# Four reorderings in a four-layer gated cross-attention kernel: combinations behind the gathering, tile 0 ahead of a meeting, norm steps, a copy

## The chip, the cores and the metric

The kernel runs on 1 core of one Trainium2 chip. The metric is the time of one execution on the device in microseconds (us); lower is better. Three runs of the kernel before took 2125.79, 2128.64 and 2129.28 us; the median is 2128.64 us.

## The reference, cut to what matters

Sixteen sequences of 56 tokens of width 256 (896 tokens, seven tiles of 128) pass through four layers. Each layer is a gated cross-attention over 16 contexts of 1500 positions of width 64, and a gated feed-forward part that is different in each layer:

```python
x = x + tanh(g_xattn[n]) * xattn_n(layernorm(x), ctx)     # n = 0..3
x = x + tanh(g_ffn[n])   * ffn_n(layernorm(x))
# ffn_0: 64 experts, top 6 (grouped router), at most 64 tokens each, relu squared, and a shared expert
xd = zeros((E, CAP + 1, D)).at[e_flat, slot].set(x[tok])           # gathering
yd = einsum('eci,edi->ecd', relu2(einsum('ecd,eid->eci', xd, w1)), w2)
out = zeros((T, D)).at[tok].add(yd[e_flat, slot] * gate)           # combination
# ffn_1: 8-bit activations, ternary weights; ffn_2: 16 experts, silu(g) * u, dense with top 6 weights
# ffn_3: rmsnorm(h), then 8 experts, top 2, and a shared expert
h = x * rsqrt(mean(x * x) + 1e-6) * rms_weight
# the end of each attention of layers 1 to 3, per tile of tokens:
out = ctx_lat.reshape(b, s, H * K) @ Wo.T                          # projection
```

Everything is computed to fp32 accuracy: a matrix product is split into three, high x high, high x low and low x high, where `H` and `L` at the end of a name mark the high and the low part.

## The kernel before

**Five programs.** TensorE, VectorE, ScalarE, GpSimd and SyncE (which issues the loads) each have a program of their own, and each runs its instructions strictly in order. They wait for one another by semaphores: `e.wait_ge(*x_out.at(n, i))` waits until `x_out` of tile i in layer n has been counted. Between two stages all five meet in `stage_end` (L968): an engine drains, adds one to `meet`, and waits until all five have done so. Whatever stands behind it on any engine waits for the last engine to come.

**Layer 0's experts.** The order of the tasks is one list, made by `sparse_order` (L226), and every engine walks it and does its own share of each task. The 64 experts go in eight groups of eight, g = 0 to 7, that is four pairs q = 4g to 4g + 3. A group is a list of fourteen steps, n = 0 to 13: `ups(g)` are the up products of the group; `pick(q)` builds on GpSimd the 0/1 selection matrix `S` of the pair (L2352, from `slot_of_t` and `slots`), which the combination uses; `disp(g + 1, 0)` and `disp(g + 1, 1)` gather the tokens of the next group on TensorE (L1666, 14 matmuls each) out of `ST` compares, `st(..., a)`, that VectorE makes (L2826) and TensorE also uses (L962 with `w_pairs`); ScalarE copies the gathered tokens out; `downs(q), downs(q + 1)` are down products, whose result VectorE and ScalarE split into `YDL` (L2846) and `YDH`; `comb(q)` adds the pair's results back to the tokens (L1709, 8 matmuls with `S`, `YDH`, `YDL`); `gturn(g + 1)` turns the gates of the next group. The combination of pair 4g + 3 stands in the group after. In the kernel before, step 6 is `comb(4g)` and step 7 is `disp(g + 1, 1)` with `st(2)`.

After every step one task of a side list is popped, which prepares the contexts of layer 1: `kt` products and subtractions (L2868 on VectorE), turns of `V` and `key_steps` (L1734 on TensorE, `key_steps` on GpSimd at L2372). `wload` and `pload` in the list are loads of weights and slots on SyncE's queue; `wload` is placed behind steps 6 and 13 by number.

**Banks.** A product of TensorE lands in one of eight PSUM banks. In the experts the upper four go round: use m takes bank 4 + m % 4 (`upper_uses`, L413), and waits until the use four before it has been copied out. Combinations add up in banks of their own; gatherings, up and down products, the turns of the gates and those of the context are uses of the upper four. `S`, `YDH` and `YDL` are rings of three: `pick(q)` waits for `comb(q - 3)`.

**Projection of the attentions.** `pe_project` (L1572) goes over the seven tiles of tokens, one product of 24 matmuls each (L962, `MH`, `ML` by `CH`, `CL`) into bank i % 3. ScalarE makes `CH` (L2025), and GpSimd or VectorE the low part `CL` (L2030, `low_part`, L2027): all tiles of layer 1 and tile 0 of the others by GpSimd, the rest of layers 2 and 3 by VectorE; in layers 1 to 3 tile 0's `CH` and `CL` are made ahead of the stage. `dve_project` (L2619) adds the product to `X`, and makes mean and scale (`mv`, `shift`, `rstd`). `TURN_BEHIND[n]` says by how many tiles TensorE's turn of the normed tokens `Y` (`pe_project_turn`, L1591, matmul with `ident`) follows the projection, `LOGITS_BEHIND[n]` the same for the router's product (`pe_logits`). In layer 3 there is a second norm: ScalarE squares (`act_square`, L2074), VectorE makes `rr` from the sums `ss`, GpSimd raises it to a power (`pool_rms`, L2318, the operation at L2321), and VectorE multiplies (L2664, in `dve_rms`, L2652) before TensorE turns the tile at L1220. GpSimd also splits weights there (`WL`, L2326). The projections of layers 1 to 3 stand behind such a meeting (L1828); the last thing that TensorE does before it is the last values product of the attention (L1551, `E`, `V`).

**Experts of layers 2 and 3.** `act_experts` (L2096) walks the list of its layer. The first task of a unit (n, c) is two products of TensorE (`pe_up`, L1613, `YH` by `WH` at L962), `up(n, c)` in the list; ScalarE takes the first of them through silu out of its bank into `R` (`act_up`, L2088, the activation at L2093), VectorE multiplies `R` by the second (L2801, `HF`). In the task `gate(n, c)` ScalarE rounds `HF` to `HH` and GpSimd makes `HL` (L2342) for the down product.

## Time and profile before

| | kernel before |
|---|---|
| runs | 2125.79, 2128.64, 2129.28 us |
| median | 2128.64 us |
| profiled execution, its own time | 2128.17 us |
| its span in the trace | 2126.4 us |
| TensorE matmuls (PE) busy | 2040.6 us, 96% |
| TensorE weight loads (PEld) busy | 1422.9 us, 67% |
| VectorE (DVE) busy | 1485.2 us, 70% |
| ScalarE (ACT) busy | 1074.6 us, 51% |
| GpSimd (POOL) busy | 1359.4 us, 64% |
| mean granted TensorE clock, share of full speed | 0.994 |

The span is the stretch from the first to the last instruction that the profiler recorded, in one execution; all places in the trace are told in us from its start. The execution's own time is 1.8 us longer. Busy shares are means over very different stages, so what an engine's time is worth must be read at the place. TensorE's ends are modelled, to some tenths of a us. In a row of a timeline the numbers are the start and the length, and the bracket at the end is how long the engine stood idle before it and which instruction's end released it.

### The profile page before, as it was taken

The page shows a single profiled execution, that of the slowest core. Times are in us where ns is not written, and L with a number is a line of the kernel's source. Part 1 is how long each engine was busy: PE and PEld are TensorE (multiplying, and loading weights), DVE is VectorE, ACT ScalarE, POOL GpSimd, SP SyncE. Part 2 cuts the span into 40 slices and gives each one's busy share as a digit, 9 for nine tenths or more (in the row PEclk, how much of TensorE's full clock was granted, in tenths as well). Part 3 has the DMA queues.
Part 4 walks back from the last instruction along what each step waited for, and adds up shares of the span by engine and source line. Part 5 has one row for each costly group of instructions (what it writes and reads, how often), then busy time and mean ns, then how long its engine had stood idle before and what let it go on. Part 6 is the DMA issues. An engine that isn't in the chain of part 4 may idle for free.

```text
span 2126.4 us, 35215 instructions
## 1 busy us (share of the span) xinstructions
PE 2040.6 (96%) x13564; PEld 1422.9 (67%) x13568; DVE 1485.2 (70%) x2141; ACT 1074.6 (51%) x1770; POOL 1359.4 (64%) x850
## 2 busy tenths in 40 slices
PE   7998999999999998999999999999999999999998
PEld 5787777765565556766555655588897655655588
DVE  6869871588888857666788888653335888888653
ACT  4552332565665656211665665544434656656543
POOL 0368873188788785454788788634441887887644
PEclk9999999999999999999999999999999999999999
DMA  3035776423223104102223222025533232231022
GB/s 99 11 119 178 248 240 202 96 59 88 59 59 88 45 31 140 26 1 63 59 64 83 59 64 68 22 79 156 149 91 78 59 88 59 59 88 45 33 54 72
DMA packets 65704, 179.59 MB, mean 84 GB/s; under 512 B 11280, under 2 KB 21280, under 8 KB 65154
## 3 DMA queue, kind: packets, MB, share of 16 engines
q1 hardware_dynamic: 65154, 177.01, 31.5%
q8 instruction: 109, 1.79, 0.4%
q14 instruction: 57, 0.47, 0.1%
q10 hardware_dynamic: 384, 0.33, 0.1%
HBM read 162.32 MB, written 14.98 MB: 83 GB/s over the span
## 4 chain that ended last, share of the span: by engine, by line
PE 80%; DVE 7%; ACT 5%; POOL 3%; issue 3%; DMA 1%; POOLq 0%; DVEq 0%; SPq 0%; ACTq 0%
PE psum L962 20%; PE psum L1551 19%; PE psum L1537 18%; PE psum L1425 5%; PE psum L1436 3%; ACT E L2011 3%; PE psum L976 3%; PE psum L1709 3%; PE psum L1568 2%; PE psum L1666 2%; PE psum L1354 1%; POOL CL L2030 1%; PE psum L1252 1%; PE psum L1232 1%; DVE ST L2826 1%
## 5 line engine op out<-in xcount | busy, mean ns | idle before, releaser
L2563 DVE TENSOR_REDUCE mx<-psum 128x2 f32<-128x1000 f32 (+1 forms) x540 | 552.5, 1066 | 164.2 <-PE psum L1425 161.7
L2292 POOL TENSOR_TENSOR SA<-SA,E 125x896 f32<-125x896 f32 x288 | 606.3, 2105 | 19.0
L2011 ACT ACTIVATE E<-psum 125x896 f32<-125x896 f32 x576 | 512.7, 918 | 101.2 <-PE psum L1537 83.2
L1551 PE MATMUL psum<-E,V 125*64 125x448 f32 x2304 | 449.4, 539 | 0.0
L1551 PEld LDWEIGHTS psum<-E,V 125*64 125x64 f32 x2304 | 163.4, 137 | 246.4 <-issue 239.0
L1537 PE MATMUL psum<-QH,KH 64*125 64x448 f32 x1152 | 255.3, 399 | 10.2 <-ACT E L2011 4.2
L1537 PE MATMUL psum<-QL,KH 64*125 64x448 f32 x1152 | 241.4, 365 | 0.0
L2292 POOL TENSOR_TENSOR SA<-E,E 125x896 f32<-125x896 f32 x48 | 101.5, 2115 | 200.3 <-PE psum L1425 152.1
L1537 PE MATMUL psum<-QH,KL 64*125 64x448 f32 x1152 | 228.1, 363 | 0.0
L1425 PE MATMUL psum<-KH,QH 64*128 64x500 f32 x864 | 182.0, 405 | 1.8 <-ACT QR L1953 1.6
L2585 DVE RECIPROCAL RS<-psum 128x448 f32<-128x448 f32 x48 | 142.0, 2957 | 46.0 <-PE psum L1568 45.5
L2342 POOL TENSOR_TENSOR HL<-HF,HH 128x448 fp32r<-128x448 f32 x70 | 81.2, 1164 | 129.9 <-ACT HH L2116 129.8
L1537 PEld LDWEIGHTS psum<-QH,KH 64*125 64x125 f32 x1152 | 111.0, 181 | 78.2 <-ACT E L2011 57.3
L1537 PEld LDWEIGHTS psum<-QL,KH 64*125 64x125 f32 x1152 | 128.7, 182 | 6.5
L2801 DVE TENSOR_TENSOR HF<-R,psum 128x448 f32<-128x448 f32 x62 | 38.3, 620 | 128.9 <-PE psum L962 109.6
L1537 PEld LDWEIGHTS psum<-QH,KL 64*125 64x125 f32 x1152 | 124.5, 183 | 3.5
L1425 PEld LDWEIGHTS psum<-KH,QH 64*128 64x128 f32 x864 | 88.2, 185 | 51.1 <-issue 35.8
L1436 PE MATMUL psum<-KH,QD 64*128 64x500 f32 x270 | 121.9, 452 | 0.0
L2000 ACT ACTIVATE OB<-psum 128x448 f32<-128x448 f32 x45 | 24.5, 545 | 183.0 <-PE psum L1551 183.0
L1991 ACT ACTIVATE M<-psum,bd 128x128 fp32r<-128x128 f32 x192 | 54.7, 367 | 119.8 <-PE psum L1510 119.8
L2292 POOL TENSOR_TENSOR SA<-SA,SB 125x896 f32<-125x896 f32 x45 | 104.3, 2319 | 14.0 <-DVE SB L2581 13.5
L2352 POOL TENSOR_SCALAR S<-slot_of_t,slots 128x896 fp32r<-128x896 bf16 x32 | 92.9, 2906 | 31.8 <-PE psum L1709 17.0
(310 smaller groups left out, 4302.1 us busy)
## 6 DMA issues: line engine op xcount, KB each, us to landing
KH<-kt_scratch SPq DMA_DIRECT2D x96, 375.0 KB, 5.3
KL<-kt_scratch SPq DMA_DIRECT2D x96, 375.0 KB, 7.1
EW<-in_f_w SPq DMA_DIRECT2D x64, 256.0 KB, 5.9
kt_scratch<-kt SPq DMA_DIRECT2D x16, 750.0 KB, 6.4
WS<-in_f_w SPq DMA_DIRECT2D x31, 384.0 KB, 4.7
GB<-gates_scratch SPq DMA_DIRECT2D x36, 224.0 KB, 3.8
slot_of_t<-slots_scratch SPq DMA_DIRECT2D x64, 112.0 KB, 4.4
WoT<-in_a_WoT SPq DMA_DIRECT2D x24, 256.0 KB, 3.4
```

The costliest lines, as they stand in the source:

```text
L962: i = e.matmul(o, a, b, start=start and n == 0, stop=stop and n == len(pairs) - 1, **kw)
L976: e.matmul(psum[:, bank, 0:P], ident[:, :], ident[:, :], start=True, stop=True)
L1425: return e.matmul(psum[:, bank, 0:CW], QH[b % 3][rows, q:q + P], KH[b % 3][rows, c * CW:(c + 1) * CW], start=c == 0, stop=True, skip_group ...
L1436: return e.matmul(psum[:, 5, 0:CW], QD[b % 2][rows, :], KH[b % 3][rows, c * CW:(c + 1) * CW], start=(c, odd) == (0, 0), stop=True, skip_gr ...
L1537: i = e.matmul(psum[0:LP, pair + odd, 0:HT], keys[rows, which], queries[rows, odd * shift:odd * shift + HT], start=kind == "head" and x == ...
L1551: i = e.matmul(psum[c * DC:(c + 1) * DC, 4, 0:HT], V[0:LP, b, tile * DC:(tile + 1) * DC], E[g[n, b, k] % NE][0:LP, half[c]], start=k == 0, ...
L2011: e.activation(E[m % NE][0:LP, :].rearrange("p (c q) -> p c q", c=2), psum[0:LP, pair:pair + 2, 0:HT], ACT.Exp).then_inc(exp_set.sem, 1)
L2292: e.tensor_tensor(SA[b % 2][0:LP, :], a[0:LP, :], x[0:LP, :], ALU.add).then_inc(sum_set.sem, 1)
L2342: e.tensor_tensor(m["HL"][u][:, :], m["HF"][u][:, :], m["HH"][u][:, :].bitcast(F32), ALU.subtract).then_inc(hl_set.sem, 1)
L2352: e.tensor_scalar(m["S"][q % 3][:, :], m["PB"][q % 3][:, :], m["slots"][:, CAP0:CAP0 + 1], None, ALU.is_equal).then_inc(s_set.sem, 1)
L2563: e.tensor_reduce(o, psum[:, max_banks(kind, *t), 0:CW], AX.X, ALU.max).then_inc(small_free.sem, 1)
L2585: e.reciprocal(RS[:, :], psum[:, small_bank(kind, b), 0:HT]).then_inc(small_free.sem, 1)
```

## The change

Four things are moved; nothing is computed in another way.

1. In each group of layer 0's experts, `comb(4g)` and the step with `disp(g + 1, 1)` and `st(2)` change places. The side list's tasks keep their step numbers, and so do the loads.
2. In layers 1 to 3 the product of projection tile 0 is issued by TensorE before the meeting instead of behind it, into bank 6 instead of bank 0, and VectorE reads it from there. Tile 3, which used to wait for tile 0 to be read out of bank 0, no longer waits.
3. In layer 3's projection the turn of a normed tile follows the projection by three tiles instead of four, the router's product by five instead of six, and GpSimd's and VectorE's steps of the second norm come one tile earlier.
4. In layer 2's experts ScalarE takes the first product of unit (2, 0) out of its bank before it takes up the rounding of unit (0, 0), instead of behind it: `R` of unit (2, 0) is made first.

```diff
@@ -258,8 +258,8 @@
         pick = lambda q: [("pick", q)] + ([("pload", q + 3)] if q + 3 < E0 // 2 else [])
         steps = [([("gsl", 0)] if g == 0 else []) + [("ups", g)] + (pick(0) if g == 0 else []), pick(q) if g > 0 else [("gturn", 0)],
                  [("comb", q - 1)] if g > 0 else [], ([("disp", g + 1, 0)] if more else []) + st(0) + (pick(1) if g == 0 else []),
-                 [("downs", q), ("downs", q + 1)], (pick(q + 1) if g > 0 else []) + st(1), [("comb", q)],
-                 ([("disp", g + 1, 1)] if more else []) + st(2), [("downs", q + 2), ("downs", q + 3)],
+                 [("downs", q), ("downs", q + 1)], (pick(q + 1) if g > 0 else []) + st(1),
+                 ([("disp", g + 1, 1)] if more else []) + st(2), [("comb", q)], [("downs", q + 2), ("downs", q + 3)],
                  pick(q + 2), [("comb", q + 1)] + st(3),
                  [("gsl", g + 1)] if more else [], pick(q + 3), [("comb", q + 2)] + ([("gturn", g + 1)] if more else [])]
         for n, step in enumerate(steps):
@@ -397,10 +397,10 @@
     return [t for t in CORES[n] if n != 2 or not ahead(t)]
 
 
-TURN_BEHIND = {0: 2, 1: 0, 2: 2, 3: 4}
+TURN_BEHIND = {0: 2, 1: 0, 2: 2, 3: 3}
 SPLIT_AT = {0: 3, 2: 1, 3: 1}
 EARLY_UP = {2: 5, 3: 4}
-LOGITS_BEHIND = {0: 2, 1: 0, 2: 3, 3: 6}
+LOGITS_BEHIND = {0: 2, 1: 0, 2: 3, 3: 5}
 TURNED_NORM = {0: 1, 2: 5, 3: 8}
 MADE = (slice(0, 3 * P), slice(3 * P, T))
 BACK = {0: ((0, 1), (2,)), 1: ((3, 4), (5, 6))}
@@ -1572,14 +1572,8 @@
     def pe_project(e, n):
         behind = TURN_BEHIND[n]
         for i in range(NT + LOGITS_BEHIND[n]):
-            if i < NT:
-                e.wait_ge(*low_flag(n, i).at(n, i))
-                if i >= 3:
-                    e.wait_ge(*x_out.at(n, i - 3))
-                pairs = []
-                for m in range(H // 2):
-                    pairs += split_pairs(CH[i % 3][:, m, :], CL[i % 3][:, m, :], MH[:, m, :], ML[:, m, :])
-                product(e, psum[:, i % 3, 0:D], pairs).then_inc(projected.sem, 1)
+            if (1 if n > 0 else 0) <= i < NT:
+                pe_project_tile(e, n, i)
             if behind and 0 <= i - behind < NT:
                 pe_project_turn(e, n, i - behind)
             if n in (2, 3) and i >= LOGITS_BEHIND[n]:
@@ -1587,6 +1581,19 @@
             if n in (2, 3) and i - behind == EARLY_UP[n]:
                 e.wait_ge(*yl_set.at(TURNED_NORM[n], 3))
                 pe_up(e, n, 0, 0)
+
+    def project_bank(n, i):
+
+        return 6 if n > 0 and i == 0 else i % 3
+
+    def pe_project_tile(e, n, i):
+        e.wait_ge(*low_flag(n, i).at(n, i))
+        if i >= 3 and (n == 0 or i > 3):
+            e.wait_ge(*x_out.at(n, i - 3))
+        pairs = []
+        for m in range(H // 2):
+            pairs += split_pairs(CH[i % 3][:, m, :], CL[i % 3][:, m, :], MH[:, m, :], ML[:, m, :])
+        product(e, psum[:, project_bank(n, i), 0:D], pairs).then_inc(projected.sem, 1)
 
     def pe_project_turn(e, n, i):
         r = TURNED_NORM[n]
@@ -1825,6 +1832,7 @@
             else:
                 pe_core(e, n, behind_rope(n, lambda t: t in first_maxima(PRODUCTS_AHEAD)))
             if n > 0:
+                pe_project_tile(e, n, 0)
                 stage_end(e, next(met))
             pe_project(e, n)
             pe_stage_end(e, next(met), 3 if n < 2 else 6, (5, 22, 6, 5)[n])
@@ -2100,11 +2108,13 @@
                 if t[0] >= 2:
                     act_split(e, f, t[0])
             elif kind == "up":
-                if not swiglu or t != [0, 0]:
+                if not swiglu or t != [0, 0] and (f, t) != (2, [2, 0]):
                     act_up(e, f, *t)
             elif kind == "gate":
                 n, c = t
                 x = 2 * n + c
+                if (f, x) == (2, 0):
+                    act_up(e, f, 2, 0)
                 if not swiglu:
                     e.wait_ge(*r_set.at(f, n, c))
                     if x >= 4:
@@ -2310,9 +2320,9 @@
             pool_scales(e, 1 + 2 * n, i)
             if n != 1 and i - SPLIT_AT[n] in (0, 1):
                 pool_split(e, n, i - SPLIT_AT[n])
-            if n == 3 and i >= 2:
-                pool_rms(e, i - 2)
-        for i in (NT - 2, NT - 1) if n == 3 else ():
+            if n == 3 and i >= 1:
+                pool_rms(e, i - 1)
+        for i in (NT - 1,) if n == 3 else ():
             pool_rms(e, i)
 
     def pool_rms(e, i):
@@ -2625,7 +2635,7 @@
                 low_part(e, n, i + 2)
             if i < NT:
                 e.wait_ge(*projected.at(n, i))
-                e.scalar_tensor_tensor(X[:, i, :], psum[:, i % 3, 0:D], tanh_g[:, n:n + 1], X[:, i, :], ALU.mult,
+                e.scalar_tensor_tensor(X[:, i, :], psum[:, project_bank(n, i), 0:D], tanh_g[:, n:n + 1], X[:, i, :], ALU.mult,
                                        ALU.add).then_inc(x_out.sem, 1)
                 e.wait_ge(*x_out.at(n, i))
                 dve_stats(e, r, i)
@@ -2652,17 +2662,17 @@
     def dve_rms(e, k):
 
         m = ffn[3]
-        i = k - 2
+        i = k - 1
         if 0 <= i < NT:
             e.wait_ge(*sq_set.at(i))
             e.tensor_scalar(m["rr"][:, i:i + 1], m["ss"][:, i:i + 1], 1.0 / D, 1e-6, ALU.mult, ALU.add).then_inc(ms_set.sem, 1)
-        i = k - 3
+        i = k - 2
         if i == 0:
             e.wait_ge(*rms_in_w.at())
         if 0 <= i < NT:
             e.wait_ge(*rms_set.at(i))
             e.scalar_tensor_tensor(Y[:, i, :], Y[:, i, :], m["rr"][:, i:i + 1], m["rw"][:, :], ALU.mult, ALU.mult).then_inc(z_set.sem, 1)
-        i = k - 5
+        i = k - 4
         if i >= 0:
             dve_turn(e, 8, i, 4 + i % 4)
```

## Rows read from the trace of the kernel before

**Rows 1.** Waits of TensorE: engine, line, waited for: us, times, longest.
```profile
PE psum L1709 <- DVE YDL L2846: 9.9, 7, 2.8
PE psum L962 <- DVEq L970: 4.9, 3, 1.6
...
PE psum L962 <- ACT R L2093: 2.4, 1, 2.4
```

**Rows 2.** Windows, layer 0's experts: stretch, length, PE, PEld, DVE, ACT, POOL busy.
```profile
175.70:247.50 71.80, 63.79 (x346) 49.05 (x345) 62.76 (x80) 25.30 (x52) 71.80 (x36) 0.93 0.74 231
248.00:345.00 97.00, 91.84 (x536) 72.37 (x534) 60.51 (x88) 31.39 (x65) 65.90 (x34) 1.00 0.78 242
```

**Rows 3.** Timeline of TensorE, first matmuls of comb(0), comb(6), comb(8), comb(10).
```profile
185.87 0.74 PE L1709 MATMUL psum<-S,YDH 128*128 128x448 f32 x1 [2.79 <-DVE YDL L2846]
...
221.49 0.45 PE L1709 MATMUL psum<-S,YDH 128*128 128x448 f32 x1
...
236.12 0.47 PE L1709 MATMUL psum<-S,YDH 128*128 128x448 f32 x1 [1.71 <-DVE YDL L2846]
...
248.00 0.45 PE L1709 MATMUL psum<-S,YDH 128*128 128x448 f32 x1
```

**Rows 4.** Chain that ended last: start, us, what; two gatherings, projection tiles 4, 5.
```profile
229.68 3.25 PE psum L1666 x14
...
238.65 4.18 PE psum L1666 x14
...
2026.88 3.90 PE psum L962 x24
...
2031.00 2.83 PE psum L962 x24
```

**Rows 5.** Timeline of GpSimd, the selection matrices of pairs 5, 6 and 9, 10.
```profile
208.69 4.28 POOL L2352 TENSOR_SCALAR S<-slot_of_t,slots 128x896 fp32r<-128x896 bf16 x1
...
217.99 3.23 POOL L2352 TENSOR_SCALAR S<-slot_of_t,slots 128x896 fp32r<-128x896 bf16 x1
...
242.51 5.02 POOL L2352 TENSOR_SCALAR S<-slot_of_t,slots 128x896 fp32r<-128x896 bf16 x2
```

**Rows 6.** Timeline of VectorE, the context's subtractions in groups 0 and 5.
```profile
184.19 1.11 DVE L2868 TENSOR_TENSOR kt<-psum,kt 64x375 fp32r<-64x375 f32 x2
...
309.71 1.11 DVE L2868 TENSOR_TENSOR kt<-psum,kt 64x375 fp32r<-64x375 f32 x2 [2.51 <-ACT kt L2161]
```

**Rows 7.** Timelines at the meetings before the projections of layers 1 and 2.
```profile
781.73 2.42 PE L1551 MATMUL psum<-E,V 125*64 125x448 f32 x12
785.76 0.39 PE L962 MATMUL psum<-MH,CH 128*128 128x256 f32 x1 [1.60 <-DVEq L970]
...
786.94 4.75 POOL L2030 TENSOR_TENSOR CL<-QR,CH 128x1024 fp32r<-128x1024 f32 x2 [5.56 <-ACT CH L2025]
...
789.38 0.39 PE L962 MATMUL psum<-MH,CH 128*128 128x256 f32 x1 [0.53 <-POOL CL L2030]
...
1389.52 0.25 PE L962 MATMUL psum<-gate_hi,YH 128*128 128x16 f32 x1 [1.04 <-DVE YL L2443]
```

**Rows 8.** Timeline of layer 3's projection, VectorE's norm and TensorE's first turn.
```profile
2021.28 0.14 DVE L2435 TENSOR_SCALAR rstd<-mv 128x1 f32<-128x1 f32 x1
...
2025.66 0.48 DVE L2664 SCALAR_TENSOR_TENSOR Y<-Y,rr,rms_w 128x256 f32<-128x256 f32 x1 [1.66 <-POOL rr L2321]
...
2026.20 0.69 PE L1220 MATMUL psum<-ident,Y 128*128 128x128 f32 x2 [2.99 <-DVE Y L2664]
```

**Rows 9.** Timeline of layer 2's experts around up(2, 0) and up(3, 0).
```profile
1427.53 0.47 PE L962 MATMUL psum<-YH,WH 128*128 128x448 f32 x1 [2.36 <-ACT R L2093]
1427.66 0.62 DVE L2801 TENSOR_TENSOR HF<-R,psum 128x448 f32<-128x448 f32 x1 [1.95 <-POOL HL L2342]
...
1431.24 0.42 DVE L2448 TENSOR_TENSOR ML<-psum,MH 128x256 fp32r<-128x256 f32 x1 [0.91 <-ACT MH L1854]
...
1432.44 0.45 PE L962 MATMUL psum<-YH,WH 128*128 128x448 f32 x1
```

## The prediction, written before the changed kernel was built or timed

> **What bounds the kernel now.** I read the table of waits of TensorE first, because TensorE is busy for 2040.6 of the 2126.4 us: the time falls only where TensorE stands still or runs at the lower clock, and the reader should see that no single wait is above 0.5% of the span. Four of its waits belong to the places that the change touches [rows 1]: the combinations of layer 0's experts wait 9.9 us in seven pieces for `YDL`; the first projection tile of layers 1 to 3 waits 4.9 us in three pieces for VectorE to reach the end of the stage; the turn of layer 3's normed tokens waits 2.99 us for `Y` [rows 8]; an up product of layer 2's experts waits 2.4 us for ScalarE's copy `R`. That is 20.2 us, 0.95%. Then come the windows of the eight expert groups of layer 0, to see who else is full there: from 175.7 to 247.5 us (groups 0 to 2) GpSimd is busy for 71.80 of 71.80 us, from 248.0 to 345.0 us for 65.90 of 97.00 [rows 2]. After that only timelines, place by place.
>
> **Part 1, combinations behind the gathering.** In each group but the last, TensorE stalls at the first combination, comb(4g), and the gathering disp(g+1,1) that follows it needs nothing of it. The stalls are 2.79 and 1.71 us in groups 0 and 2 [rows 3], and 0.97, 1.88, 0.39, 1.40 and 0.73 us in the others (with these two the 9.9 us of [rows 1]). A gathering takes 3.25 us at 2.4 GHz [rows 4], more than any of the stalls, so wherever it may start at once it covers the whole stall. Whether it may start hangs on its PSUM bank, which it takes from the use four places back. In groups 1, 2, 3, 4 and 6 that use is by then the previous gathering or the up product, copied out long before. In groups 0 and 5 it is a turn of the context, which VectorE frees with the second of two `kt` subtractions: at 184.19 + 1.11 = 185.30 us, and at 309.71 + 1.11 = 310.82 us [rows 6]. TensorE would be there at 183.1 and 310.0, so there only some 0.5 us each is won. Sum: 0.97 + 1.71 + 1.88 + 0.39 + 0.73 + 2 x 0.5 = 6.7 us. In group 2 the stall is followed by a stretch at 1.2 GHz, where a gathering takes 4.18 instead of 3.25 us and half of the combination before it is slow too [rows 4]; without the stall that is up to 1.6 us more: 8.3 us.
>
> GpSimd does not let all of it through. It builds the selection matrices `S` and has no gap until 247.5 us. `S` of comb(6) ends at 217.99 + 3.23 = 221.22 us and comb(6) starts at 221.49 [rows 3, 5]: 0.27 us is all that may be kept up to there, and what groups 0 and 1 give (1.5 us) comes back as a wait for `S`. `S` of comb(10) ends at 242.51 + 2.51 = 245.02 us against a start at 248.00 [rows 3, 5]: at most 2.98 us is kept by then, of the 0.27 + 1.71 + 1.6 = 3.6. In group 3 another 1.88 us comes, less about 1 us for `S` and for the `kt` chain of VectorE, which moves only as far as the others let it (this is chosen between 0 and 2); in group 4 0.3, in groups 5 and 6 0.5 + 0.7. I take 2.98 + 1.88 - 1.0 + 0.3 + 0.5 + 0.7 = 5.4, less 0.8 for the weights and slots that must land earlier (no row shows it; between 0 and 2, near the lower end since TensorE waits for no load here) = **4.6 us gained**. Bounds: 1 us, if GpSimd's timeline binds beyond group 2, and 8.3 us. What moves along: comb(4g) ends later by 3.25 us less the stall, and behind it stand GpSimd's `S` of comb(4g+3) and ScalarE's `YDH`. In group 5 that `S` starts right at comb(20)'s end, but comb(23) is 11 us later, so nobody waits. The ST compare on VectorE and the copy of the gathered tokens on ScalarE overtake one step of the context; no DMA changes its place in SP's queue. In group 7 nothing is gathered and comb(28) only changes places with a fold product: nothing, as TensorE has no gap there.
>
> **Part 2, tile 0 of the projection ahead of the meeting (layers 1 to 3).** Today TensorE ends its last values product at 781.73 + 2.42 = 784.15 us, waits 1.60 us for the other engines, and does tile 0 from 785.76 [rows 7]. A tile takes 2.83 us from start to start, 3.1 to its last end [rows 4]. Moved ahead, tile 0 runs from 784.0 to 787.1, and only then does TensorE reach the meeting. All five engines wait there, so the meeting moves from 785.73 to about 787.1: **1.4 us later**. Queued behind it are ScalarE's `CH` of tile 1 and then GpSimd's `CL` of tile 1, which starts 1.2 us after the meeting and takes 2.37 us; tile 1 waits for that already today, at 789.38 [rows 7]. So tile 1 starts at 789.38 + 1.4, and the work moved ahead is bought with a gap of 3.6 us behind it. In layer 2 the first gate product waits 1.04 us for VectorE's chain that begins at the meeting [rows 7], and in layer 3 the turn waits for the same chain [rows 8], so the 0.4 us by which their tiles 1 to 3 come nearer to the meeting is lost there. Cost: 3 x 1.4 = **4.2 us lost**. Bounds: 2.8 us, if TensorE's end is modelled too late by half a microsecond, and 8 us, if the new gaps of 3.6, 2.4 and 2.4 us each bring the lower clock and nothing behind them hides it. I stay with 4.2, since what is slow at the start of these stages is followed by waits that absorb it. That tile 3 no longer waits for its bank and tile 0 uses bank 6 costs nothing: tile 3 doesn't wait now, and bank 6 is idle after the last maxima.
>
> **Part 3, norm steps one tile earlier (layer 3).** Today the normed tile 0 (L2664) comes in the slot after tile 3's statistics, at 2025.66, and TensorE waits 2.99 us for it [rows 8]. After the change that slot carries tile 1 and the slot before it, after tile 2's statistics at 2021.28 + 0.14 [rows 8], tile 0. TensorE then turns tile 0 at about 2021.9 instead of 2026.20, does tile 4, and waits again for tile 1's norm, which is still held by GpSimd (`rr`, behind its `WL` of block 1) until the same 2025.66. So tile 5 starts where it starts now. What is won is the turn of tile 1 (0.35 us), and the slow clock of tile 5, 3.90 against 2.83 us [rows 4], if the gap that is cut in two (some 2.6 and 1.3 us) does not lower the clock again at a place where it counts. From there to the stage's end TensorE is full. VectorE's new wait for the squares of tile 0 holds only the cast of the gate weights, 1 us before it would idle anyway. I take **0.9 us gained**, between -0.5 and 2.
>
> **Part 4, the U copy (layer 2's experts).** TensorE's 2.36 us for `R` goes, as ScalarE can make it at about 1422 instead of 1426.96, before it waits for the gate. Next late is `HL` of GpSimd (VectorE waits for it to 1427.66) for the down product, and after it the bank of up(3,0), free at 1431.24 + 0.42 = 1431.66, where up(3,0) starts now at 1432.44 [rows 9]. So 0.78 us at most is kept: **0.7 us gained**, between 0 and 2.4.
>
> **Sum.** -4.6 + 4.2 - 0.9 - 0.7 = -2.0 us. The profiled execution took 2128.17 us, so 2126.2; the median 2128.64 is 0.47 above it: **2126.6 us**, 0.1% less. Less than about 0.2% (4.3 us) a measurement of this kernel can't tell from no change: three runs of it lie 3.5 us apart.
>
> **Rivals.** (a) *GpSimd does not bind*: its `S` took 4.28 us beside VectorE's work and 2.51 us alone [rows 5], and if the new order spreads the two better, part 1 gives its 8.3 us and parts 3 and 4 their upper half: 2128.6 - 8.3 - 2.2 + 4.2 = 2122.3. For it: 15 us of GpSimd's time there are such stretching. Against: the same instructions meet in the same time. (b) *GpSimd is the bound of layer 0's groups*: its whole timeline up to group 4 stands, the stalls for `YDL` become stalls for `S`, and part 1 gives only what lies behind it, about 1.6 us; 2128.6 - 1.6 - 1.6 + 4.2 = 2129.6. For it: 71.80 of 71.80 us; against: the gaps from 248 us on [rows 2]. The Trainium skill (Perfetto Trace Analysis, Identifying the Most-Contended Engine) would have me take the busy share of GpSimd at face value and TensorE's not, and gain nothing while GpSimd is full; by that rule the time is this rival's. The same notes (GPSIMD Engine Reference, Key points) say that GpSimd shares its SBUF interfaces with VectorE's instructions of two SBUF inputs; if that is the stretching, (a) would need VectorE to do less, not the same earlier. (c) *The meeting costs more than the stalls give*, slower: the gaps of 3.6, 2.4 and 2.4 us behind tile 0 end in the lower clock, as the stall of 1.71 us did in group 2. At 1.07 us for a slow tile [rows 4], and two slow tiles in each layer, that is 4.2 + 6.4 = 10.6 us lost against 1.6 + 4.6 = 6.2: 2133.0. It decides if tile 1 and tile 2 both start at half clock and the chain of VectorE or GpSimd isn't later than they are. (d) *Part 1 does nothing*, if the gathering waits for its bank in all groups: 2126.6 + 4.6 = 2131.2; the order of the bank uses speaks against it.
>
> **Chances.** Forecast 0.50 (2124.4 to 2129.0); (a) 0.22; (b) 0.14; (c) 0.10; (d) 0.04. The range that should hold 8 in 10 reaches to the middle of (a) and of (c): 2121.5 to 2132.0. Faster by over 0.2% (below 2124.4): (a) nearly whole and a tail of the forecast, 0.28. Slower by over 0.2% (above 2132.9): half of (c) and a bit of (d), 0.07. Within: 0.65.
>
> **What would show it.** Part 1: TensorE's wait for `YDL` falls from 9.9 to about 2 us (groups 0 and 5, before the gathering now), and a wait for `S` of 1 to 2 us stands at comb(6). Part 2: no wait before tile 0, but waits of some 3.6 and 2.4 us before tile 1, and the distance from the last values product to tile 1's start grows by 1.4 us in each layer. Part 3: waits of about 2.6 and 1.3 us for `Y` instead of 2.99. Part 4: no wait for `R`, and one of 1 to 2 us behind it. I am wrong if the meeting does not move, if comb(6) doesn't wait, or if the clock falls at other places for more than 7 us.

## The result and the profile after

| | before | after |
|---|---|---|
| median of the runs taken side by side | 2126.97 us (6 runs) | 2133.90 us (6 runs) |
| ratio | | 1.0032, 95% interval 1.0017 to 1.0047 |
| profiled execution, its own time | 2128.17 us | 2135.80 us |
| its span | 2126.4 us | 2134.0 us |
| TensorE busy | 2040.6 us | 2046.9 us |
| mean granted clock | 0.994 | 0.991 |

The changed kernel is slower by 0.32%, 6.9 us. The forecast was 2 us less than before (2126.6), with a range that ended at 2132.0.

Where the time goes is read from VectorE. It runs the same 2504 recorded instructions in both kernels (those of its sequencer counted in), so the start of its n-th instruction after, less that of the n-th before, can be taken everywhere. This difference is called the shift in what follows. It is worked out from the two traces, in us, at places of the span of before (medians over five instructions; nothing is changed ahead of 130 us, so the first entry is the scatter of the start):

```
place of before   130    500    780 |  830    880  1375 | 1412 | 1427  1445  2000 | 2012   2124
shift after      0.40  -0.07  -0.12   2.01   4.17  4.19   6.56   6.11  7.07  7.02   8.50   7.61
```

Part 1 (130 to 500) gains 0.5 us. The projections of layer 1 (780 to 830) and of layer 2 (1375 to 1412) lose 2.1 and 2.4, the meeting of layer 3 (2000 to 2012) 1.5, of which part 3 gives 0.9 back. Part 4 (1412 to 1445) gains 0.45 and loses 0.96. Between 830 and 880, where nothing was changed, another 2.2 is lost.

In the waits of TensorE after (columns as in [rows 1]) the 9.9 us for `YDL`, the 4.9 for the meeting and the 2.4 for `R` are gone, and this stands in their place:

```profile
PE psum L962 <- POOL CL L2038: 3.8, 1, 3.8
...
PE psum L1673 <- DVE kt L2878: 3.0, 2, 2.1
...
PE psum L962 <- DVE kt L2878: 2.7, 2, 2.5
PE psum L962 <- SPq L970: 2.6, 1, 2.6
PE psum L962 <- DVE CL L2038: 2.6, 1, 2.6
PE psum L1220 <- DVE Y L2674: 2.4, 2, 1.6
...
PE psum L1716 <- POOL S L2362: 2.2, 3, 1.2
...
PE psum L962 <- DVE ML L2458: 1.9, 1, 1.9
```

The 3.8, 2.6 and 2.6 us are the gaps behind tile 0 in the three projections. The place in layer 1, of TensorE, SyncE's queue and GpSimd (answers to [rows 7]):

```profile
781.55 2.42 PE L1551 MATMUL psum<-E,V 125*64 125x448 f32 x12
783.91 0.39 PE L962 MATMUL psum<-MH,CH 128*128 128x256 f32 x1
...
787.08 1.29 SPq L1085 DMA_DIRECT2D wq<-wq_scratch  x3
...
788.28 2.35 POOL L2038 TENSOR_TENSOR CL<-QR,CH 128x1024 fp32r<-128x1024 f32 x1 [7.02 <-ACT CH L2033]
...
790.78 0.55 PE L962 MATMUL psum<-MH,CH 128*128 128x256 f32 x1 [3.78 <-POOL CL L2038]
791.14 0.42 PE L962 MATMUL psum<-ML,CH 128*128 128x256 f32 x1
791.35 0.41 PE L962 MATMUL psum<-MH,CL 128*128 128x256 f32 x1
```

The meeting is over at 787.08 instead of 785.73, `CL` of tile 1 starts 1.2 us behind it, tile 1 at 790.78 instead of 789.38, and its products take 0.41 us each where those of tile 0 took 0.28: the lower clock. From the end of TensorE's last values product (784.15 us before, 783.97 after) to the end of the meeting it is 1.6 us before and 3.1 us after, and the traces give the same two numbers in layers 2 and 3. So the meeting comes 1.5 us later in each of the three layers.

In layer 0's groups the two waits for the selection matrix `S` that the prediction placed are there, at comb(6) and comb(10):

```profile
221.15 0.44 PE L1716 MATMUL psum<-S,YDH 128*128 128x448 f32 x1 [0.57 <-POOL S L2362]
...
245.13 0.45 PE L1716 MATMUL psum<-S,YDH 128*128 128x448 f32 x1 [0.45 <-POOL S L2362]
```

comb(10) comes 2.87 us earlier than in [rows 3], against 2.98 forecast. But in groups 4 and 5 it is lost: comb(15) is still 2.9 us early, comb(19) is 1.5 us late. The chain that ended last has a DMA there, where the chain of before had TensorE:

```profile
271.24 3.22 POOL S L2362
277.65 9.93 DMA kt_scratch<-kt
295.11 2.94 PE psum L962 x7
```

`kt_scratch<-kt` is the store (`cstore`) with which SyncE writes a finished context's keys to memory. There are two buffers `kt`, so ScalarE's copies of context b wait until the store of context b - 2 has landed. ScalarE's copies before, then after:

```profile
276.96 0.97 ACT L2161 ACTIVATE kt<-psum 64x375 fp32r<-64x375 f32 x2 [2.99 <-DMA kt_scratch<-kt]
...
287.22 0.97 ACT L2161 ACTIVATE kt<-psum 64x375 fp32r<-64x375 f32 x2 [1.67 <-DMA kt_scratch<-kt]
```

```profile
276.62 0.98 ACT L2171 ACTIVATE kt<-psum 64x375 fp32r<-64x375 f32 x2 [6.97 <-DMA kt_scratch<-kt]
...
287.67 0.97 ACT L2171 ACTIVATE kt<-psum 64x375 fp32r<-64x375 f32 x2 [5.00 <-DMA kt_scratch<-kt]
```

The copies start within 0.5 us of where they did before; only the waits have grown, from 2.99 and 1.67 to 6.97 and 5.00 us. ScalarE came earlier, the store did not. SyncE's queue after shows what is issued ahead of each of the two stores, 1 MB of weights in four loads (`EW`):

```profile
263.92 2.01 SPq L1137 DMA_DIRECT2D EW<-in_f_w  x4
266.36 0.33 SPq L1157 DMA_DIRECT2D kt_scratch<-kt  x1
...
275.60 2.01 SPq L1137 DMA_DIRECT2D EW<-in_f_w  x4
277.65 0.43 SPq L1157 DMA_DIRECT2D kt_scratch<-kt  x1
```

### The profile page after: what moved, and what is told of

Read it like the earlier page. It is cut to its first block, busy times and chain, and to the rows that moved or that the text cites. A ratio compares the mean times of both kernels' runs of the same rounds, so it can differ in the third digit from the quotient of the medians.

```text
span 2134.0 us, 35216 instructions
## 1 busy us (share of the span) xinstructions
PE 2046.9 (96%) x13568; PEld 1425.6 (67%) x13568; DVE 1484.9 (70%) x2141; ACT 1075.7 (50%) x1770; POOL 1360.1 (64%) x850
## 4 chain that ended last, share of the span: by engine, by line
PE 76%; POOL 6%; DVE 5%; ACT 5%; issue 3%; DMA 2%; SPq 0%; PEld 0%; PEldq 0%; POOLq 0%; DVEq 0%; ACTq 0%
PE psum L962 20%; PE psum L1551 19%; PE psum L1537 18%; PE psum L1425 5%; PE psum L1436 3%; ACT E L2019 3%; PE psum L976 3%; PE psum L1568 2%; POOL S L2362 1%; PE psum L1716 1%; PE psum L1354 1%; PE psum L1673 1%; PE psum L1232 1%; POOL key_steps L2382 1%; PE psum L1252 1%
## 5 line engine op out<-in xcount | busy, mean ns | idle before, releaser
L1537 PE MATMUL psum<-QH,KH 64*125 64x448 f32 x1152 | 255.4, 400 | 10.2 <-ACT E L2019 4.0
```

The source lines that it names most:

```text
L1537: i = e.matmul(psum[0:LP, pair + odd, 0:HT], keys[rows, which], queries[rows, odd * shift:odd * shift + HT], start=kind == "head" and x == ...
```

## The experiments

Each kernel's median is of 7 to 12 runs. Ratios are to the kernel before on the same chip in the same rounds, with 95% intervals; in us they are taken of 2127.

### Each part alone

Diffs: the hunks of the change that belong to the part, on the kernel before.

> Only part 1 (comb(4g) behind disp(g+1,1)), all else as before. Theory K (the stores of the context's keys bind): TensorE is 2.9 us ahead by comb(11), as in the changed kernel, and gives all of it back by comb(18), because ScalarE's kt of context 11 and 12 still waits for the same store kt_scratch to land; the time is within 1 us of before (-0.5 us). Rival P (the predicted sum holds and part 1's gain was only lost in the changed kernel by something that parts 2 to 4 brought): 4.6 us less than before. Rival H (part 1 brings a stretch at the lower clock of its own at 295 us): 1 to 2 us more than before.

> Only part 3 (norm steps and turns one tile earlier in layer 3). Theory: TensorE waits twice (2 and 1 us) instead of once 2.99 us, and the projection of layer 3 ends 0.5 to 1.5 us earlier: 0.9 us less than before, too little to be told from no change. Rival: the gap cut in two brings the lower clock at a place where TensorE is full, 0.5 to 1 us more than before.

> Only part 2 (projection tile 0 ahead of the meeting, layers 1 to 3). Theory M (meeting later and clock): the meeting comes 1.4 us later in each layer and tile 1 waits 3.8, 2.6 and 2.6 us; tile 1 then runs at 1.2 GHz in at least two of the layers, which costs about 1 us each more, and one more stretch at the lower clock follows some 70 us behind in layer 1; together 5 to 8 us more than before. Rival N (only the later meeting costs, what follows absorbs the slow tiles): 4.2 us more. Rival O (the changed kernel's loss came from elsewhere): within 1 us of before.

> Only part 4 (R of unit (2,0) ahead of HH of unit (0,0)). Theory: the wait for R goes, but the load of the gates GB, which VectorE waits for, lands at the same time, so 0.45 us is won by 1426 us of the span, as in the changed kernel, and then the stretch at 1.2 GHz, which lay in TensorE's wait, falls where TensorE is full and takes 0.9 us: within 0.5 us of before. Rival (the prediction): 0.7 us less.

| kernel | median | ratio | in us |
|---|---|---|---|
| part 1 alone | 2126.39 | 0.9993 (0.9983 to 1.0004) | -1.5 (-3.6 to +0.9) |
| part 2 alone | 2134.25 | 1.0032 (1.0020 to 1.0043) | +6.8 (+4.3 to +9.1) |
| part 3 alone | 2125.99 | 0.9994 (0.9983 to 1.0004) | -1.3 (-3.6 to +0.9) |
| part 4 alone | 2127.43 | 1.0000 (0.9989 to 1.0010) | 0.0 (-2.3 to +2.1) |

(Median of before 2127.13.) Part 2 alone has a loss of the size of the whole; no other part can be told from no change. Part 1 alone shows the same course as in the changed kernel: comb(11) 3.2 us early, comb(19) 1.9 us late, ScalarE's two copies of `kt` at 276.60 and 288.03 us. In the trace of part 4 alone 0.8 us is won between 1412 and 1445 us, as forecast; its whole time doesn't show it.

### Part 1: what takes the 2.9 us back

The first pair of kernels, with part 1 and without it, puts loads of weights behind the stores; the second pair takes bytes away.

```diff
+    for first in (36, 40, 44, 48):              # at the end of sparse_order
+        batch = [("wload", e) for e in range(first, first + 4)]
...
+        while order[at][0] != "cstore":
+            at += 1
+        at += 2 if order[at + 1][0] == "cload" else 1
+        order[at:at] = batch
```

> Part 1, and in SyncE's list the four batches of weight loads for experts 36 to 51 stand behind the next store of the context's keys (and the context load that goes with it) instead of ahead of it; nothing is left out. Theory K (the store kt_scratch lands late because 1 MB of weights is issued ahead of it): the two stores that took 10 us to land take 5 to 7, ScalarE's kt no longer waits 5 and 7 us, and TensorE keeps the 2.9 us of groups 0 to 2 and some of its stalls of groups 4 and 5: 3 to 4.5 us less than before. Rival G (VectorE or GpSimd would be late at the same place anyway): what part 1 gives alone, 0.7 us less than before. Rival W (the weights come late instead and the up products of groups 4 to 6 wait): 1 us or more above before.

> The moved loads alone, combinations as before. Theory K: before, only 0.8 us of TensorE's time at 295 us hangs on the store, and the rest is stalls for YDL, so 0 to 1 us less than before. If it gives as much as the run with both (3 us or more), then part 1 has no part in that gain.

Measured: with part 1 ratio 1.0009 (0.9997 to 1.0020), 1.9 us more than before, but with an interval that takes in no change; alone 1.0010 (1.0001 to 1.0019), 2.1 us more. The mechanism of rival W is there. The stores land in 5.3 and 5.8 us, and ScalarE's two long waits for them are gone, but the weights are late instead: TensorE waits in the up products of group 4, where it had no wait for weights in the trace of before.

```profile
277.68 3.68 PE L970 MATMUL psum<-XD,EW 128*128 128x64 f32 x16 [3.13 <-DMA EW<-in_f_w]
```

So here the order of the queue only chose who was late.

The second pair loads only the first half of the weights of experts 32 to 47, the up weights; their down weights are left out.

```diff
-                e.dma_start(m["EW"][x % 12][:, :], io["f0_w"][NS0 + x])...
+                cut = 256 if 32 <= x < 48 else 512
+                e.dma_start(m["EW"][x % 12][:, 0:cut], io["f0_w"][NS0 + x][:, 0:cut])...
```

> Part 1, and of the weights of experts 32 to 47 only the first half (the up weights) is loaded, so the outputs of those experts are not computed with their own down weights; all else is as before. Theory K2 (in groups 3 and 4 the DMA engines are the bound: context stores and weight loads together fill them, and whichever is issued later lands late): both land in time, TensorE keeps the 2.9 us of groups 0 to 2 and adds stalls of groups 3 and 4; against the run with half loads alone it is 3 to 4.5 us faster. Rival G (VectorE and GpSimd bind there): the gap between the two is the 0.7 us that part 1 gives with full loads.

> Half loads of experts 32 to 47 alone (only their up weights are loaded, the down weights are left out), combinations as before. Theory K2: TensorE's stalls for YDL stay, only the 0.8 us wait for kt at 295 us goes: 0 to 1 us less than before. Rival: DMA binds before too, then 2 us or more less.

Measured: part 1 with half loads 0.9974 (0.9964 to 0.9984), 5.5 us less than before; half loads alone 0.9999 (0.9990 to 1.0007), nothing. The gap is 5.3 us (2.5 to 8, an estimate from the two intervals), where part 1 with full loads gives 1.5: K2 as told, and somewhat above its 3 to 4.5. comb(17), 1.5 us early with part 1 alone, is 4.0 us early, and comb(31), 0.3 us late with part 1 alone, is 5.9 us early. The two stores took this long from their issue to their landing:

| kernel | store issued at 266 to 267 us | store issued at 277 to 280 us |
|---|---|---|
| before | 10.2 us | 7.2 us |
| after | 10.2 us | 9.9 us |
| part 1 alone | 10.3 us | 10.5 us |
| part 1, loads behind | 5.3 us | 5.8 us |
| part 1, half loads | 6.6 us | 4.2 us |

The windows of part 1 alone and of part 1 with half loads from 255 to 300 us (stretch, length, PE, PEld, DVE, ACT, POOL busy, clock, DMA share, GB/s):

```profile
255.00:300.00 45.00, 39.36 (x214) 29.56 (x214) 35.83 (x50) 16.81 (x35) 37.39 (x21) 0.96 0.75 235
```

```profile
255.00:300.00 45.00, 44.16 (x265) 34.83 (x264) 40.45 (x55) 17.57 (x37) 43.01 (x22) 1.00 0.59 197
```

TensorE is busy 44.16 instead of 39.36 of 45 us, with GpSimd at 43.01. ScalarE's one wait of over 1 us for a store in this window is this; it ends 4 us earlier than with full loads:

```profile
272.56 0.97 ACT L2162 ACTIVATE kt<-psum 64x375 fp32r<-64x375 f32 x2 [2.71 <-DMA kt_scratch<-kt]
```

### Part 2: the late meeting, the gap, the clock

There are six kernels. `c_early_count` and `c_count_only` count TensorE at the meeting first:

```diff
             if n > 0:
-                pe_project_tile(e, n, 0)
-                stage_end(e, next(met))
+                e.drain().then_inc(meet.sem, 1)
+                pe_project_tile(e, n, 0)
+                e.wait_ge(meet.sem, 5 * next(met))
```

`c_early_count` and `c_parts_only` make tile 1's parts before the meeting too, and in layers 2 and 3 GpSimd makes the `CL` of tile 1 there instead of VectorE (parts of the edit, comments added):

```diff
-        return n == 1 or i == 0 or (n == 0 and i % 2 == 0)
+        return n == 1 or i == 0 or (n == 0 and i % 2 == 0) or (n > 1 and i == 1)    # low_by_pool
...
                 act_part(e, n, 0)        # ScalarE, before stage_end, n > 0
+                act_part(e, n, 1)        # waits for the last scores and for o_divided(n, 4)
...
                 low_part(e, n, 0)        # GpSimd, before stage_end
+                low_part(e, n, 1)
```

The filled kernels `c_filled` and `c_filled_fit` are part 2 with `pe_stage_end(e, next(met), 0, BUSY[n])` behind tile 0, which lets TensorE make throw-away products while it waits at the meeting, and `late_meeting` has `pe_busy(e, 6, 13)`, 13 such products, ahead of `stage_end` in the kernel before.

> The kernel before, and in layers 1 to 3 TensorE does 13 throw-away products (0.232 us each, 3.0 us) between its last values product and the meeting, so that it comes to the meeting 1.4 us after the others, as in part 2, but without a gap behind tile 0 and with nothing moved. Theory M (the meeting's delay has a price of its own): 3 x 1.4 = 4 us more than before, and what part 2 takes beyond that (to 7.1) is the gap behind tile 0 with its slow tiles. Rival Q (the delay is absorbed behind the meeting, part 2 loses by the gaps alone): within 1 us of before. Rival R (the delay costs all): 7 us more.

Measured: 2133.12 against 2127.16, ratio 1.0024 (1.0014 to 1.0034), 5.1 us more (3.0 to 7.2). The delay alone, with no gap and nothing moved, costs most of what part 2 costs: theory M, and a little above its 4. The meeting is over 3.15 us behind the last values product in each layer, 1.55 us later than before, and the shift grows by 1.6, 1.6 and 1.5 us in the three layers: in this trace a late meeting costs just its delay. The last values product, the fill, tile 0 and tile 1 in layer 1:

```profile
782.11 2.42 PE L1551 MATMUL psum<-E,V 125*64 125x448 f32 x12
784.47 3.17 PE L976 MATMUL psum<-ident 128*128 128x128 f32 x26
787.90 0.36 PE L962 MATMUL psum<-MH,CH 128*128 128x256 f32 x1 [0.26 <-PEq L970]
791.35 0.39 PE L962 MATMUL psum<-MH,CH 128*128 128x256 f32 x1 [0.38 <-POOL CL L2031]
```

> TensorE counts itself at the meeting, then does tile 0, then waits; CH and CL of tile 1 stay behind the meeting. Theory M: the meeting is back at its time, tile 1 starts at 789.4 as before (it waits for its CL), so nothing is lost and nothing won but for a gap of 2.3 us: within 1 us of before. Rival S (gap and slow tiles are most of part 2's loss): 2 to 3 us more, as these stay.

Measured: 1.0004 (0.9994 to 1.0014), 0.9 us more. With the meeting at its own time the loss is gone, though tile 1 still waits in a gap of 2.12 us in layer 1 and runs slowly there, and tile 4 of layer 2 runs slowly too (4.2 and 4.3 us from the first to the last start of a matmul, where it is 2.6 to 2.8 at full clock). This is M; the 2 to 3 us of S are at the upper end of the interval (-1.3 to 3.0).

> Part 2 as in the change, and TensorE does 28, 19 and 19 throw-away 128x128 products (0.12 us each) while it waits for tile 1 in layers 1, 2 and 3. The waits stay, only the clock is kept up. Theory M: what part 2 costs beyond the later meeting is slow tiles, so the time is 4 to 5 us more than before instead of 7.1. Rival L (the loss is all in late parts and chains, and the clock costs nothing): 7 us more, as part 2 alone.

> As the filled run, with 16, 11 and 11 throw-away products: one takes 0.232 us, not 0.12, so that 28, 19 and 19 took 6.5, 4.4 and 4.4 us and pushed tile 1 back by 2.7, 1.8 and 1.8 us. Theory M: with the fill inside the gaps tile 1 starts where it starts in part 2 alone and at 2.4 GHz: 1 to 3 us more than before, where part 2 alone takes 7.1 more. Rival L (the push back was hidden by GpSimd's chain, and the clock doesn't count either): 3.9 us more, as with the longer fill.

Measured: 1.0018 (1.0010 to 1.0027), 3.8 us more, with the long fill; 1.0029 (1.0018 to 1.0041), 6.2 us more, with the fitted one. The rows of the two in layer 1:

```profile
786.60 6.51 PE L977 MATMUL psum<-ident 128*128 128x128 f32 x56
```

```profile
788.41 3.83 PE L977 MATMUL psum<-ident 128*128 128x128 f32 x32
792.11 0.35 PE L963 MATMUL psum<-MH,CH 128*128 128x256 f32 x1
```

A throw-away product is two matmuls of the record, 0.232 us, which the first expectation had taken as one. The fitted fill does keep the clock in layers 1 and 2: by the shifts they cost 1.6 and 1.5 us, those of part 2 alone 3.0 and 3.0. That would be 2.9 us for the slow tiles (in part 2 alone tile 1 of layer 1 and tile 4 of layer 2). The timed runs do not bear it out (6.2 against 6.8 us, the intervals overlap nearly whole), since the stretches at the lower clock elsewhere differ from execution to execution: in the profiled one of the fitted fill, 3.7 us were lost between 830 and 880 us and 3.1 won back by 1000. How much of part 2's loss is slow tiles stays open, between 0 and 3 us.

> CH and CL of tile 1 made before the meeting in layers 1 to 3, tile 0 behind the meeting as before. Theory M: tile 1 follows tile 0 without the 0.5 us wait, and GpSimd and VectorE are 1.2 to 2.4 us less busy behind the meeting: 0.5 to 2 us less than before; with the early count it gave 3.3. Rival: it gives all of the 3.3 alone, and moving tile 0 is worth nothing even with the meeting untouched.

Measured: 1.0008 (0.9985 to 1.0031), which tells nothing: one of its twelve runs took 2152.80 us, at a granted clock of 0.943, so that its median is 1.6 us below before's while its ratio is above 1 and the interval spans 10 us. By the shifts its trace gains 1.1 us in layer 1 and nothing in layers 2 and 3.

> Part 2 made otherwise: TensorE counts itself at the meeting first, then does tile 0 and only then waits; and ScalarE's CH and GpSimd's CL of tile 1 are made before the meeting in layers 1 to 3. Theory M (part 2 lost because the meeting waited for TensorE, and the parts of tile 1 hang on the meeting): the meeting falls back to VectorE's time, tile 1 follows tile 0 at once, and TensorE's waits of 3.8, 2.6 and 2.6 us are gone; each layer's projection starts 1.6 us earlier than before: 2 to 5 us less than before. Rival V (the chain of VectorE and GpSimd behind the meeting binds the projection anyway): within 1 us of before.

Measured: 0.9983 (0.9973 to 0.9993), 3.6 us less. Tile 0 moved ahead pays once the meeting doesn't wait for it and tile 1 is ready: by the shifts 2.4 us in layer 1, 1.1 in layer 2 and nothing in layer 3. As the early parts alone gained 1.1 us of this in their trace, and their timed runs decide nothing, how the 3.6 us divide between the early parts and the moved tile isn't shown.

### What is left of it all

> Parts 1 and 3 with the early count version of part 2, without part 4. If the places add, 0.7 + 1.1 + 3.3 us, 5 us less than before. Rival: what is won shifts the stretches at the lower clock to places where TensorE is full, and only 2 to 3 us remain.

Measured: 2123.11 against 2127.42, ratio 0.9979 (0.9970 to 0.9988), 4.5 us less than before and some 11 less than the changed kernel. Its median is the lowest of the kernels that leave nothing out. Parts 1 and 3 added 0.9 us to the 3.6 of the early count, not 1.8 to 2.8; the difference is within the intervals.

## Why the prediction was wrong, step by step

**What bounds the kernel.** Right: all that moved, moved through TensorE's waits or its clock. The places of the change make 5.1 of the 7.6 us between the spans; 2.2 were lost between 830 and 880 us, where nothing was changed and the granted clock was 0.97 instead of 1.00, and 0.4 is the scatter of the start. One reading was wrong: a single wait was above 0.5% of the span, 11.9 us for the load of `Wv` (0.56%), which the change doesn't touch.

**Part 1.** Right within the scatter of a trace (0.4 us at its start) up to group 2: group 0 gives about 0.5, comb(6) and comb(10) wait for `S`, comb(10) is 2.87 us early (2.98). The wait at comb(6) is 0.57 us, not 1 to 2. Wrong from group 3 on: group 3 adds nothing of its 0.9, and groups 4 and 5 lose 4.4 us. The failing step is the 0.8 us, "between 0 and 2", for what must land earlier, with the 1.0 for `S` and the `kt` chain: no row was behind them. The step asked whether TensorE waits for loads, and in layer 0's groups it doesn't. ScalarE waits for a store, and that wait stood in the trace of before with 2.99 and 1.67 us, unread, because ScalarE is 51% busy and these waits cost nothing then. The `kt` chain that I charged with 1 us "of VectorE" is held by this store. When TensorE came 2.9 us earlier the wait took it all. The half loads show it: with the bytes taken away part 1 gives 5.3 us, where 5.4 less the 0.8 for the loads was forecast; with all bytes it gives 1.5 instead of 4.6. Groups 5 and 6 gave what was said for them, 1.3 us (comb(27) is 0.2 us late, comb(19) 1.5).

**Rival (b)** named the right size for part 1 (1.6 us) with the wrong resource, so its size was luck. The Trainium skill's rule (Perfetto Trace Analysis, Identifying the Most-Contended Engine), taken as no gain while GpSimd is full, is not what happened: GpSimd was busy for 71.61 of 71.80 us from 175.7 to 247.5 us and TensorE was 2.9 us ahead at the end. What was short was the time of the DMA, with a share of 0.79 and 0.92 in the 9.9 us before each of ScalarE's two late copies (0.81 and 0.96 in the same stretches of before, 0.63 and 0.52 with part 1 and half loads). The Trainium skill says that on each DMA engine descriptors are consumed in ring order (DMA: Bandwidth & Descriptors, Queues, rings and completion order). The traces agree as far as they show this: a store of 0.75 MB behind 1 MB of weights took 9.93 us to land, and 5.3 and 5.8 us with those loads behind it. Half loads alone, in the window from 255 to 300 us, have a DMA share of 0.55, against the 0.75 of full loads in part 1 alone:

```profile
255.00:300.00 45.00, 42.34 (x239) 32.67 (x238) 39.49 (x50) 18.12 (x38) 40.68 (x22) 1.00 0.55 194
```

With half the bytes and without part 1, TensorE is busy for 42.34 us there: the room is there, and it takes part 1 to use it (44.16).

**Part 2.** The mechanism was right in each point: the meeting late, the gaps of 3.8, 2.6 and 2.6 us (forecast 3.6, 2.4 and 2.4), tile 1 at 790.78 (forecast 790.78). The failing step is the size of the term: 3 x 1.4 = 4.2 us forecast, 6.8 (4.3 to 9.1) measured. The meeting is late by 1.5 us per layer, not 1.4, and the late meeting by itself measured 5.1 us (3.0 to 7.2) for a delay of 3 x 1.55, 4.7 by its shifts. So some 4.5 of the 6.8 us go with the delay; this is an estimate from these delays. What the other 2.3 are isn't shown. The prediction set the slow tiles behind the gaps to nothing ("followed by waits that absorb it"). Tile 1 ran mostly at 1.2 GHz in all three layers of the changed kernel (4.1 us from the first to the last start of a matmul instead of 2.7, granted clock 0.65 to 0.68), and by the shifts of part 2 alone 2.9 us were not absorbed. Against that, the fitted fill, which keeps the clock, ran in 6.2 us more, and the kernel that only counts early has two more slow tiles than before and ran in 0.9 us more. The bound of 8 us held it.

**Part 3.** Forecast 0.9; the last stretch of the changed kernel's trace gives 0.9 and that of part 3 alone 1.0, but its runs, 1.3 us less (-0.9 to 3.6), can't tell it from nothing. The gap was cut in two as told, with waits of 1.63 and 0.81 us in the changed kernel (2.4 in all) instead of 2.6 and 1.3, where one of 2.99 was before.

**Part 4.** Right in the trace of part 4 alone: `HL` is next late (0.99 us), then the bank of up(3, 0) (1.93 us), and 0.8 us is won, against 0.7. What the prediction didn't name is that `HL` hangs on VectorE's `HF`, which waits for the load `GB` until it lands. In the changed kernel 0.45 us was won, and a stretch at the lower clock, from 1428.4 us before, came from 1438.8 us, where TensorE is full, and took 0.9. Over the runs it is nothing.

**The sum.** -2.0 forecast, +6.8 measured, 8.8 apart. By the parts measured alone, part 1 missed by 3.1 us, part 2 by 2.6, parts 3 and 4 by 0.3. The 2.8 us left are no more than the intervals of four separate measurements; in the profile 2.2 of them lie between 830 and 880 us. Rival (c) had the right sign, at 0.10, and its 2133.0 is 0.9 us from the median, but by luck: it charged part 2 with 10.6 us (6.8 measured) and credited the other parts with 6.2 (2.8 measured alone).

## What to carry over

When a stall of the bounding engine is taken away, look for every wait on the other engines in the next 50 us, also the ones that cost nothing today, and above all those on a DMA. Here the instructions came 2.9 us earlier and the landings moved by less than 0.5 us, so the wait for them became the new bound. A barrier is reached by its last engine: work moved ahead of it is free only up to that engine's idle time (here 1.6 us for a tile of 3), unless the engine counts itself first. And the inputs of the next piece must be moved as well, or the gap only changes its place.

## What the runs showed of the hardware

In layer 3's projection VectorE's `CL` and GpSimd's `WL` do not run side by side: the later one takes longer by about what the first has left. `CL` takes 1.22 us alone; started in the middle of GpSimd's `WL` (1.85 us) it takes 2.03, and where it starts first, `WL` takes 2.90. Part 2 alone, then the long fill:

```profile
2022.17 1.85 POOL L2334 TENSOR_TENSOR WL<-WS,WH 128x768 fp32r<-128x768 f32 x1 [0.45 <-ACT WH L2094]
...
2023.07 2.03 DVE L2038 TENSOR_TENSOR CL<-QR,CH 128x1024 fp32r<-128x1024 f32 x1 [1.96 <-ACT CH L2033]
```

```profile
2024.16 1.23 DVE L2039 TENSOR_TENSOR CL<-QR,CH 128x1024 fp32r<-128x1024 f32 x1 [0.50 <-ACT CH L2034]
2024.21 2.90 POOL L2335 TENSOR_TENSOR WL<-WS,WH 128x768 fp32r<-128x768 f32 x1
```

Who comes first by 0.05 us decides who is delayed by about 1 us. This agrees with the Trainium skill (GPSIMD Engine Reference, Key points), which has GpSimd contend with VectorE's instructions of two SBUF inputs. It is also one difference between the long fill and part 2 alone in layer 3, where the last tile of the long fill's projection started 2.4 us earlier in relation to the last values product. Another is tile 5, which ran slowly in part 2 alone (4.3 us) and not in the long fill (2.7). How much either gives wasn't tried.

And the same gap doesn't always bring the lower clock: behind 2.6 us in layer 2 tile 1 took 4.07 us from the first to the last start of a matmul in the changed kernel and 2.68 in part 2 alone. Nor does the lower clock come at the same place: the feed-forward part of layer 1 ran with the granted clock at 1.00 in the profile of before from 855 to 866 us and at 0.84 after, with nothing changed there but that all comes 2 us later. Before, then after:

```profile
855.00:866.00 11.00, 10.39 (x92) 9.20 (x91) 7.45 (x25) 5.16 (x12) 4.07 (x6) 1.00 0.01 2
```

```profile
855.00:866.00 11.00, 9.20 (x68) 7.75 (x69) 7.84 (x27) 2.97 (x8) 4.30 (x6) 0.84 0.14 41
```

Part 1 alone, which changes nothing there either, lost 2.0 us at the same place in its profile, part 2 alone 0.3. One profile of this kernel is therefore good for the waits but not for a sum to 2 us.
